# Sixteen score maxima computed a batch row ahead, in the expert stretch, and the softmax V product in one piece

## What is computed

```python
xn = layernorm(x)                       # x is (8, 512, 128)
# branch s: 16 causal heads of width 8, weight 1 - tanh(energy)^2 in place of softmax
attn = 1 - tanh((mask(q k^T) - threshold) / tau) ** 2
s = (attn / attn.sum(-1) @ v) @ Wo.T
# branch g: a transformer block with 16 softmax heads, not causal, and 8 experts (top 2) plus a shared one
h = rmsnorm(xn) ; X = xn + softmax(q k^T / sqrt(8)) @ v @ wo
h2 = rmsnorm(X) ; combine = top-2 weights of softmax(h2 @ router)
g = silu(X + shared(h2) + sum_e combine_e * expert_e(h2))
return x + s * g
```

## Time and profile before

| | |
|---|---|
| median of 3 runs | 1172.4 us (1167.02 to 1173.9) |
| the profiled execution | 1171.43 us |
| its span in the trace | 1169.6 us |
| busy share of the span | PE 90%, DVE 72%, ACT 55%, PEld 42%, POOL 29% |
| mean granted TensorE clock | 0.953 |

### The profile page before, as it was taken

How to read it: one execution, slowest core, us unless ns; L and a number is a source line. 1 busy time by engine, 2 the same in 40 slices (tenths; PEclk the granted TensorE clock), 3 DMA queues, 4 the chain that set the end, 5 groups by cost and what they waited for, 6 DMA issues and landing times.

```text
span 1169.6 us, 18848 instructions
## 1 busy us (share of the span) xinstructions
PE 1055.8 (90%) x7112; PEld 487.0 (42%) x7112; DVE 839.3 (72%) x1692; ACT 648.9 (55%) x873; POOL 340.6 (29%) x178
## 2 busy tenths in 40 slices
PE   3469999899999899999999999989999999999998
PEld 1112465224651356424553246523464235532465
DVE  7366887659767687677876598765976868764872
ACT  4038842597227972388524983269722786248822
POOL 6500354005430335203351045301542033510023
PEclk9559999999998999999998999999999999989999
DMA  5530244104420045202350034400442012610020
GB/s 176 108 59 2 63 117 70 29 2 88 126 37 28 22 76 130 52 2 50 83 118 28 3 73 111 66 28 3 95 122 41 21 40 58 143 29 1 2 73 10
DMA packets 71787, 69.68 MB, mean 60 GB/s; under 512 B 8528, under 2 KB 63056, under 8 KB 71568
## 3 DMA queue, kind: packets, MB, share of 16 engines
q1 hardware_dynamic: 68928, 64.41, 25.0%
q10 hardware_dynamic: 2768, 4.06, 1.0%
HBM read 53.37 MB, written 14.81 MB: 58 GB/s over the span
## 4 chain that ended last, share of the span: by engine, by line
PE 66%; ACT 13%; DVE 12%; issue 4%; DMA 2%; SPq 2%; POOL 1%; ACTq 0%; POOLq 0%; DVEq 0%
PE O L977 12%; PE O L993 10%; ACT PT L534 7%; PE S L1009 6%; DVE PT L685 6%; PE M L919 6%; PE S L1011 6%; PE S L1010 6%; PE S L952 6%; PE M L916 5%; DVE nmax L648 3%; PE M L902 2%; ACT L534 2%; PE M L1082 2%; PE M L908 1%
## 5 line engine op out<-in xcount | busy, mean ns | idle before, releaser
L534 ACT ACTIVATE PT<-S 128x1024 f32<-128x1024 f32 (+1 forms) x448 | 420.0, 972 | 100.7 <-PE S L952 98.9
L648 DVE TENSOR_REDUCE nmax<-M 128x1 f32<-128x512 f32 x512 | 332.8, 685 | 121.1 <-PE M L916 75.5
L685 DVE SCALAR_TENSOR_TENSOR PT<-PT 128x768 f32<-128x768 f32 (+1 forms) x192 | 215.6, 1170 | 95.6 <-ACT PT L534 95.2
L977 PE MATMUL O<-PT,V 128*12 128x256 f32 (+3 forms) x2816 | 251.1, 438 | 0.0
L409 POOL TENSOR_TENSOR split<-split,parts 128x512 f32<-128x512 f32 x32 | 91.1, 2846 | 463.3 <-ACT parts L495 463.3
L952 PE MATMUL S<-stackQ,stackK 64*128 64x512 bf16 (+3 forms) x1024 | 202.1, 356 | 21.3 <-DMA stackQ<-mTZ 7.3
L568 ACT ACTIVATE PT<-S 128x1024 f32<-128x1024 f32 x72 | 73.9, 1027 | 257.9 <-PE S L1011 257.8
L424 POOL TENSOR_TENSOR PT<-PT,CB 128x1024 f32<-128x1024 f32 x56 | 133.3, 2387 | 283.7 <-DMA CB<-scrC 175.0
L1009 PE MATMUL S<-h2hi,wgu_hi 128*128 128x512 f32 x288 | 151.4, 526 | 0.0
L993 PE MATMUL O<-PT,wdn 128*128 128x512 f32 x288 | 142.8, 595 | 0.0
L916 PE MATMUL M<-KX,stackQ 128*128 128x512 bf16 x256 | 105.6, 414 | 26.0 <-DMA KX<-scrK 22.8
(11 more groups left out here) (177 smaller groups left out, 1034.8 us busy)
## 6 DMA issues: line engine op xcount, KB each, us to landing
CB<-scrC SPq DMA_DIRECT2D x64, 256.0 KB, 5.4
stackQ<-scrQ SPq DMA_DIRECT2D x192, 64.0 KB
stackK<-scrK SPq DMA_DIRECT2D x192, 64.0 KB
scrQ<-parts SPq DMA_DIRECT2D x16, 384.0 KB, 4.5
scrK<-parts SPq DMA_DIRECT2D x16, 384.0 KB, 8.7
KX<-scrK SPq DMA_DIRECT2D x96, 32.0 KB
PT<-in_w_gu ACTq DMA_DIRECT2D x2, 1152.0 KB, 7.8
xin<-in_x SPq DMA_DIRECT2D x8, 256.0 KB, 3.0
```

Source lines behind the costliest of these rows:

```text
L534: a.activation(PT[:, n % SLOTS, 2 * q * w:2 * q * w + 2 * w].rearrange("p (r n) -> p r n", r=2), S[k][:, :].rearrange("p (r n) -> p r n", ...
L648: v.tensor_reduce(nmax[:, h % 2, h // 2, t:t + 1], M[k][:, :], AX.X, ALU.max, negate=True).then_inc(m_read[k], 1)
L685: v.scalar_tensor_tensor(p, p, 1.0, p, ALU.subtract, ALU.mult).then_inc(weighed, 1)
L977: last = t_.matmul(O[k][32 * q:32 * q + VW, i0:i1], V[:, j, 4 * g + q, :], PT[:, n % SLOTS, w * q + at:w * q + at + i1 - i0], start=(j == ...
```

## The change

- Run Y moves from the row's own softmax stretch into the expert stretch of the batch row before, like X: 48 maxima there in place of 32, all from KX, whose copy DMAs grow from four to six head pairs. X is spread over experts 1 to 6 (before: 2 to 8), Y over 6 to 8. `maxT_X` stands in expert 7, `maxT_Y` at the end of expert 8.
- Run Z keeps to the softmax stretch and is spread over units 1 to 8, two or three to a unit.
- The first batch row has no row before it: there the pairs 4 and 5 are done in its softmax stretch as run F, beside Z. The last row prepares nothing.
- In a softmax unit the two score pieces stand at the first two slots, and the V product is one piece of 512 queries in the third, in place of two pieces of 256 in the second and fourth. The first unit of each head group had one piece already.
- DVE's `early` part for expert 1 becomes three quarters of its list.

```diff
-RUNS = {"X": (0, 4), "Y": (4, 6), "Z": (6, 8)}
+RUNS = {"X": (0, 4), "Y": (4, 6), "F": (4, 6), "Z": (6, 8)}
...
-spread(MAX["Y"], {0: 1, 1: 4, 2: 4, 3: 4, 4: 3})
-spread(MAX["Z"], {4: 1, 5: 3, 6: 4, 7: 4, 8: 4})
-PLACES[5].insert(2, "maxT_Y")
+spread(MAX["F"], {0: 1, 1: 4, 2: 4, 3: 4, 4: 3})
+spread(MAX["Z"], {1: 1, 2: 2, 3: 2, 4: 2, 5: 2, 6: 3, 7: 2, 8: 2})
+PLACES[5].insert(0, "maxT_F")
...
-spread(MAX["X"], {EXPERT + e: n for e, n in enumerate((0, 0, 5, 4, 4, 5, 6, 6, 2))})
+spread(MAX["X"], {EXPERT + e: n for e, n in enumerate((0, 4, 6, 6, 6, 6, 4))})
+spread(MAX["Y"], {EXPERT + 6: 2, EXPERT + 7: 7, EXPERT + 8: 7})
...
-PLACES[END - 1] += ["maxT_X"]
+PLACES[EXPERT + 7].insert(2, "maxT_X")
+PLACES[END - 1] += ["maxT_Y"]
...
-        KX = sb("KX", [128, 2, RUNS["X"][1], L], bf16)
+        KX = sb("KX", [128, 2, RUNS["Y"][1], L], bf16)
...
-                    early = len(work) * 4 // 6 if e > 1 else 2
+                    early = len(work) * 4 // 6 if e > 1 else len(work) * 3 // 4
...
                     for i in range(4):
-                        if i % 2 == 0:
-                            if n:
-                                scores(it, n, i // 2)
+                        if n < N1:
+                            if i < 2 and n:
+                                scores(it, n, i)
+                            elif i == 2 and n in v_at:
+                                with_v(it, v_at[n])
+                        elif i % 2 == 0:
+                            scores(it, n, i // 2)
```

More of the change, by code:

```diff
@@ L50, in width @@
     return L if kind == "all" else sum(L - 128 * j for j in js)
-MAX = {run: [("max", 2 * hp + r, t) for hp in range(*pairs) for t in range(NT) for r in range(2)] for run, pairs in RUNS.items()}
+MAX = {run: [("first" if run == "F" else "max", 2 * hp + r, t) for hp in range(*pairs) for t in range(NT) for r in range(2)] for run, pairs in RUNS.items()}
 EXPERT, END = UNITS, UNITS + NE
@@ L90, with __init__ @@
 PLACES[EXPERT + 5].insert(2, "proj1")
-PLACES[END - 1] += ["maxT_X"]
+PLACES[EXPERT + 7].insert(2, "maxT_X")
+PLACES[END - 1] += ["maxT_Y"]
 PLACES[END] += ["outT"]
-AHEAD = {"xnT", "hT", "Q2", "K2", "V2", "Q1", "K1", "V1", "maxT_X", *MAX["X"]}
+AHEAD = {"xnT", "hT", "Q2", "K2", "V2", "Q1", "K1", "V1", "maxT_X", "maxT_Y", *MAX["X"], *MAX["Y"]}
+FIRST_ROW = {"maxT_F", *MAX["F"]}
 class Uses:
-    def __init__(self, own, following, before=(0, 0)):
-        self.places = {n: [w for w in work if (following if w in AHEAD else own)] for n, work in PLACES.items()}
+    def __init__(self, own, following, before=(0, 0), first=False):
+        done = set() if own else {"maxT_Y", *MAX["Y"]}
+        self.places = {n: [w for w in work if (first if w in FIRST_ROW else following if w in AHEAD else own) and w not in done]
+                       for n, work in PLACES.items()}
         self.order = [w for n in sorted(self.places) for w in self.places[n]]
@@ L119 @@
 FIRST = Uses(False, True)
-LOOP = Uses(True, True, FIRST.total)
-LAST = Uses(True, False, LOOP.row(B - 1).before)
+ROW0 = Uses(True, True, FIRST.total, True)
+LOOP = Uses(True, True, tuple(f + r for f, r in zip(FIRST.total, ROW0.total)))
+ROWS = [ROW0] + [LOOP.row(it - 1) for it in range(1, B - 1)] + [Uses(True, False, LOOP.row(B - 2).before)]
 S_USES = UNITS + NE
@@ L375, in _ @@
             prepare(FIRST, 0)
-            for it in range(B - 1):
-                row(LOOP.row(it), it, True)
-            row(LAST, B - 1, False)
+            for it in range(B):
+                row(ROWS[it], it, it < B - 1)
         @block.gpsimd
@@ L719, in take @@
                 k, _n = u(name)
-                if name[0] == "max":
+                if name[0] in ("max", "first"):
                     maximum(u, name)
```

45 lines of the change are left out of this document (20 added, 25 removed).

## The result

| | before | after |
|---|---|---|
| median | 1173.15 us (1167.02 to 1177.7, 4 runs) | 1225.69 us (1220.51 to 1231.21, 4 runs) |
| ratio of after to before | | 1.0464, 95% interval 1.043 to 1.0499 |
| profiled execution, span | 1171.43, 1169.6 | 1231.21, 1229.5 |
| softmax stretch, mean of rows 2 to 8 | 41.17 | 36.98 |
| second attention stretch | 38.70 | 38.71 |

What follows compares the result with a forecast made beforehand. PE was taken to bound the expert stretch, PE's wait for DVE's reads of maxima the softmax stretch. Sum: 1171.4 + 7 x (8.8 - 4.0) + 2 = 1207.0 us, range 1193 to 1219.

Steps and rivals of the forecast that it cites:

- Expert stretch, +8.8 a row forecast: Expert stretch of seven rows: 3.9 of added PE work plus 5.0 of new waits, taken as 8.8 us a row.
- Work of 3.9: PE in the expert stretch: sixteen maxima at 0.23, 3.7 us, and one more transpose of maxima at 0.24.
- The stop before `maxT_Y`: End of expert 8: PE waits 1.5 us for DVE's maxima, mult and split, 0.8 more than before.
- The pairs behind a mult: Experts 3, 5 and 7: PE waits 0.5 us for an M buffer behind DVE's mult, three times, 1.6 together.
- 0.4, 0.6 and 0.8: Experts 1 and 2: PE's waits for routing weights, third and fourth maximum, and the one after; 1.9 us together.
- Softmax stretch, -4.0 forecast: Softmax stretch: fewer maxima and the new order save 4.4 us a row, less half clock; taken as 4.0.
- The half clock at a row's start: Start of the softmax stretch: PE at half clock for two units in most rows, each 1.6 us above ACT's pace.
- First row, +2 forecast: First row's softmax stretch: six maxima in units 2 and 3 make DVE late; +2 us, from 0 to +4.
- KX copies at nothing: Twelve KX copies grow by half but are issued during the second attention stretch, so were costed at nothing.
- 1: Expert stretch: DVE keeps up, PE pays 3.9 and the softmax stretch gives 6.0; 1158 us, chance 0.07.
- 2: Expert stretch: half the waits, 2.5 against 5.0, as DVE reads earlier; 1183 us, chance 0.17.
- 3: Expert stretch: PE's clock falls in the new stops, doubling 4.4 us a row; 1238 us, chance 0.08.

Runs made afterwards that it cites:

- e3: Changed kernel with POOL's weighting of experts 1 to 7 cut to 8 of 512 columns, no list changed; 1205.12 us, ratio 1.0263.
- e10: Kernel of e7 with the branch s blocks of expert 3 and X's split moved in DVE's order, apart from POOL's weighting; 1195.76 us, ratio 1.02.
- e11: Kernel before with PE's product for 16 of X's maxima issued twice into the same buffer, DVE reading once; 1196.16 us, ratio 1.0188.
- e5: Changed kernel with the double item of experts 2 to 8 in PE's first step instead of its last; 1226.91 us, ratio 1.0474.
- e1: Kernel before with the new order of the softmax units alone, all maxima left where they were; 1185.24 us, ratio 1.0108.
- e2: Changed kernel with the old order of the softmax units, maxima moved as in the change; 1216.47 us, ratio 1.0377.
- e7: Changed kernel with old softmax unit order, first-row K2 copies of four head pairs, and four maxima per unit in the first row; 1214.92 us, ratio 1.0357.
- e6: Changed kernel with DVE's reads of Y's 16 maxima in the expert stretch cut to 128 of 512 columns; 1215.43 us, ratio 1.0372.

## Why the prediction was too low

Against its own sum (1171.4 + 33.6 + 2 = 1207; the profiled execution took 1231.2):

- **Expert stretch, +8.8 a row forecast, +10.63 measured: the step that failed.** I took DVE's durations from rows where it had SBUF to itself. "Expert 3 also has two blocks of branch s on DVE, 0.9 to 1.2 each, ahead of its maxima: 0.4" was priced at a block's length, and X's split not at all. The change brings both beside POOL's weighting. X's split now stands behind expert 6's mult, whose product POOL weights. The blocks keep their place behind expert 2's mult, but that mult comes 2.6 later (17.1 after the stretch's start, 14.5 before), and POOL's weighting of expert 2 does not (20.4 to 20.9, before 20.9 to 21.2): DVE reaches the first block at 20.5 in place of 17.9, about when the weighting starts, and this block or the second runs beside it. With the split that costs 2.6 a row (e3), of which 2.1 come back by moving them away (e10). PE's stops in the second row were 1.64 in expert 3, where the sum had 0.4, and 0.65 and 0.29 at X's split, where it had nothing:

```profile
338.03 0.39 PE L913 MATMUL M<-KX,stackQ 128*128 128x512 bf16 x1 [1.64 <-DVE h2T L670]
...
365.95 0.22 PE L922 MATMUL M<-identb,mhX 128*64 128x128 bf16 x1 [0.65 <-DVE nmax L651]
366.46 0.39 PE L913 MATMUL M<-KX,stackQ 128*128 128x512 bf16 x1 [0.29 <-DVE nmax L651]
```

The sign was in the trace before, on DVE (line 671 is 674 now). In expert 1 POOL was idle, in expert 3 a POOL operation of 1.17 ran (308.89 to 310.06), and in the last row the weighting itself (line 424):

```profile
303.56 0.29 DVE L671 TENSOR_TENSOR ht<-h2T,rden 128x128 f32<-128x128 f32 x1
...
309.55 0.66 DVE L671 TENSOR_TENSOR ht<-h2T,rden 128x128 f32<-128x128 f32 x1
...
1137.33 2.02 DVE L671 TENSOR_TENSOR ht<-h2T,rden 128x128 f32<-128x128 f32 x1
...
1136.80 2.39 POOL L424 TENSOR_TENSOR PT<-PT,CB 128x1024 f32<-128x1024 f32 x1 [1.36 <-DVE PT L792]
```

- **The rest of that sum was 0.8 too high.** With POOL's weighting cut (e3) the stretch takes 57.49 + 8.0. Work of 3.9 was 3.5 and 0.24 (e11; the earlier trace rows). The stop before `maxT_Y` was forecast as 1.5 and is 1.5. The pairs behind a mult (1.6) were no separate price: moving them returned nothing (e5). What they stand for is that DVE, busy 55.25 of 68.50, is late in one expert or in the next. Not counted was that the first product behind a stop adds its whole 0.39 to the chain (342.04 above), while one in a stream adds only the 0.23 between two ends (343.13): an estimated 0.16 more for each of the seven stops that end at such a product, 1.1 of the 5.3 by which PE's busy time grew. As printed, two parts of the sum are also 0.1 too high: three times 0.5 is 1.5, and 0.4, 0.6 and 0.8 make 1.8.
- **Softmax stretch, -4.0 forecast, -4.19 measured: right in size, by two errors.** I gave the new order 0.85 of it; it costs 0.9 to 1.3 (e1, e2). The moved maxima alone bring 5.1, more than the rest of the forecast gave them. That the size came out is luck. The half clock at a row's start, which I had expected for two units in most rows, is there; in the third row (columns as above):

```profile
386.00:390.00 4.00, 3.29 (x14) 0.59 (x18) 0.82 (x2) 4.00 (x5) 0.00 (x0) 0.52 0.27 81
```

- **First row, +2 forecast, +5.95 measured.** The end of that range was +4. Six reads in a unit at the row's start, not the order, made it (e7: 43.0 against 47.7 in e2, both with the old order).
- **KX copies at nothing.** In rows 2 to 8 they are hidden behind the second attention stretch: PE waits for KX once in the whole execution, in the opening. There nothing covers them: the opening is 10.1 longer in the profiled execution, where PE's wait for KX grew from 22.8 to 25.7 and that for X's rows from 4.3 to 10.2; on the mean of the executions it is about 4, not clear of their scatter.
- **Rivals.** 1 and 2 wanted fewer waits than forecast; there were more. 3 fell: the clock is 1.00 in the stretch, with its stops of 1.64 and 1.47, and in the slice with PE at 2.37 of 4.

Together: 7 x (10.63 - 4.19) = 45.1 in place of 33.6 is 11.5; the first row 4.0, the opening 10.1 and the last row -1.3 make it 24.3, against the 24.2 us between 1207 and the profiled execution. That execution is the longest of the four; on the medians the miss is 18.7.

The 1.2 to 1.4 us lost in each of the intervals 0-1 and 1-2, where neither POOL nor Y's reads play a part, are the price of X's new spread by the second row's trace: five maxima more stand ahead of expert 2's last gate/up half (5 x 0.217 = 1.1 by e11), PE stops there for 0.24 (the routing weights), 0.21 and 0.65 (DVE's reads), and two of the stops add their 0.16: 2.5 of the 2.6. No run took these apart.

What stays open: how much the opening costs on the mean; the split of the waits beyond what e3 and e6 take away; and what a third M buffer would change, which no run tried.

## What to carry to other kernels

Idle time of an engine that serves a full one is no room: DVE's 42.49 busy of 57.43 looked like 15 us free, and 9.6 us of reads cost PE 7, 2.6 of them through POOL; the rest fits two buffers that tie each read to a moment, which is argued from the waits and not tested. Before work is moved onto an engine's list, look at what the move pushes its other operations against on a third engine, and at what merely comes later by it: a duration read where POOL was idle (0.29) did not hold beside POOL (up to 2.50). And weigh a gain by its last unit: half of the move brought two thirds of the softmax gain.

## What the runs showed of the hardware

- A DVE operation with two SBUF inputs (line 674) took 0.29 alone and up to 2.50 beside a POOL operation of 2.37; a cast 0.17 and 1.40, in e6 1.97. The maxima, from PSUM, kept to 675 to 693 ns all through, and DVE's reciprocal on SBUF (line 672) to 241 to 246 ns, beside POOL or not.
- POOL did not pay for it there: its weighting took 2.37 and 2.40 beside the two slow operations of DVE, 2.39 on the mean of all 56. Elsewhere it is POOL that is long: in the second attention stretch one operation of line 414 took 7.88, beside seven of DVE's on PT (line 688) that kept their 0.95 and 1.22; the same operation took 1.16 in the expert stretch. No run took this apart.

```profile
306.97 7.88 POOL L414 TENSOR_TENSOR split<-split,parts 128x512 f32<-128x512 f32 x1 [13.15 <-ACT parts L499]
...
331.37 1.16 POOL L414 TENSOR_TENSOR split<-split,parts 128x512 f32<-128x512 f32 x1
```

- A product of PE took 0.39 from start to end both behind a stop and in a stream (342.04 and 342.97), as the profile models its end; in a stream the ends lie 0.23 apart, so that a stop costs about 0.16 beyond its idle time.
